# First attention of a transformer block: couples of maxima moved behind the values, the row of maxima by 32-row matmuls, reciprocals in quarters

## The reference

```
x = x + attn(layernorm(x), W_qkv, b_qkv, W_out, b_out)    # H=16 heads of D=64
x = x + ffn(layernorm(x), ...)                            # 16 heads of 8, then 4 experts

def attn(x, ...):
    q, k, v = split(x @ W_qkv + b_qkv)                    # (b, s, 3, H, D)
    k = k + pos_enc
    scores = einsum('bqhd,bkhd->bhqk', q, k) / 8
    out = einsum('bhqk,bkhd->bqhd', softmax(scores), v)
    return out.reshape(b, s, H * D) @ W_out + b_out
```

## Time and profile before

| | |
|---|---|
| median of 3 runs | 2605.41 us |
| the profiled execution | 2604.06 us |
| its span, first to last instruction | 2602.3 us, mean granted TensorE clock 0.969 |
| TensorE matmuls busy | 2437.0 us (94%) |
| VectorE busy | 1970.0 us (76%) |
| ScalarE busy | 1119.5 us (43%) |
| GpSimd busy | 1007.9 us (39%), all of it in the first 1500 us |

### The profile page before, as it was taken

One profiled execution on the slowest core, in us unless ns is written; L12 is line 12 of the kernel. 1 busy time (PEld: TensorE's weight loads), 2 busy tenths in 40 slices (PEclk: granted clock), 3 DMA queues, 4 the chain that ended last, 5 costly groups with the idle time before them and its releaser, 6 DMA issues. The chain is left out here.

```text
span 2602.3 us, 37556 instructions
## 1 busy us (share of the span) xinstructions
PE 2437.0 (94%) x13217; PEld 1300.1 (50%) x13217; DVE 1970.0 (76%) x3109; ACT 1119.5 (43%) x1178; POOL 1007.9 (39%) x459
## 2 busy tenths in 40 slices
PE   5999999999999999999999789999998999999696
PEld 3555454555454555555555344454454455445465
DVE  6767777777767676777777498888987988888834
ACT  0333343333343343443344305556565556655332
POOL 1676767675867767676757600000000000000000
PEclk8999999999999999999999859999999999999898
DMA  2000000000000000000000000000000000000000
GB/s 83 1 1 1 1 1 1 1 1 1 1 1 1 1 1 1 1 1 1 1 1 1 17 8 5 5 12 5 5 8 7 9 8 5 5 5 12 17 0 16
DMA packets 17395, 16.59 MB, mean 6 GB/s; under 512 B 4656, under 2 KB 13760, under 8 KB 17088
## 3 DMA queue, kind: packets, MB, share of 16 engines
q1 hardware_dynamic: 17216, 14.20, 2.0%
HBM read 8.16 MB, written 1.05 MB: 4 GB/s over the span
## 5 line engine op out<-in xcount | busy, mean ns | idle before, releaser
L715 ACT ACTIVATE prob<-scores 128x1024 f32<-128x1024 f32 x512 | 523.9, 1025 | 765.4 <-PE scores L408 717.4
L798 POOL TENSOR_TENSOR accp<-accp,prob 128x1024 f32<-128x1024 f32 x320 | 773.5, 2417 | 71.7 <-ACT prob L715 35.2
L982 DVE TENSOR_REDUCE mxp<-ring 128x1 f32<-128x512 f32 x1024 | 634.9, 680 | 151.5 <-PE ring L383 151.5
L743 ACT ACTIVATE prob<-scores 128x1024 f32<-128x1024 f32 x512 | 496.7, 1022 | 417.5 <-PE scores L567 417.3
L420 PE MATMUL acc_o<-prob,v 128*64 128x512 f32 x2048 | 496.7, 606 | 0.0
L531 PE MATMUL ring<-khi,klo_q 128*128 128x512 f32 x1104 | 450.2, 452 | 8.7 <-DVE accs L1130 3.8
L1107 DVE TENSOR_REDUCE mxp<-ring 128x1 f32<-128x512 f32 x576 | 372.1, 686 | 37.5 <-PE ring L531 37.3
L1107 DVE TENSOR_REDUCE accs<-ring 128x1 f32<-128x512 f32 x528 | 343.6, 687 | 52.9 <-PE ring L531 52.2
L531 PEld LDWEIGHTS ring<-khi,klo_q 128*128 128x128 f32 x1104 | 214.4, 195 | 312.1 <-DVE mxp L1107 132.4
L403 PE MATMUL scores<-klo_q,khi 64*128 64x512 f32 x2048 | 354.5, 418 | 0.0
L567 PE MATMUL scores<-klo_q,khi 128*128 128x512 f32 x1028 | 338.2, 410 | 7.0 <-issue 6.4
(11 more groups left out here) (119 smaller groups left out, 1520.9 us busy)
## 6 DMA issues: line engine op xcount, KB each, us to landing
klo_q<-stage_q SPq DMA_DIRECT2D x72, 64.0 KB, 2.0
w_all<-w_pairs SPq DMA_DIRECT2D x1, 1344.0 KB, 10.6
klo_q<-m_rows SPq DMA_DIRECT2D x68, 2.0 KB
pos_sb<-pos SPq DMA_DIRECT2D x1, 1024.0 KB, 5.9
mrow<-m_rows SPq DMA_DIRECT2D x64, 2.0 KB
v<-w SPq DMA_DIRECT2D x1, 1024.0 KB, 5.2
prob<-w SPq DMA_DIRECT2D x4, 256.0 KB, 3.6
out<-prob SPq DMA_DIRECT2D x4, 256.0 KB, 2.4
```

The costliest lines, as they stand in the source:

```text
L715: nc.scalar.activation(prob[:, T % SLOTS1, :, :], sc[T % 2][:, :, :], ACT.Exp, scale=SCALE1).then_inc(exp_done, 1)
L743: nc.scalar.activation(prob2[:, u, t % 4, :, :], sc[u][:, :, :], ACT.Exp, scale=SCALE2).then_inc(exp2_done[u], 1)
L798: nc.gpsimd.tensor_tensor(accp[:, k % 2], accp[:, k % 2], prob[:, T % SLOTS1], ALU.add).then_inc(pool_acc, 1)
L982: done(nc.vector.reduce_max(mxp1[k % 2][:, h * QT + q, kc:kc + 1], bank[:], AX.X), ("max", k, q, kc, h))
```

## The change

1. `scores(T)` no longer adds the maxima. A new `maxima_off(T)`, called once for two tiles and ahead of them, starts the accumulation of all four banks by four matmuls of 32 rows: `onesw` has ones in rows 0, 32, 64 and 96, and `mrow` holds the row of maxima in those four rows. It waits for the exp of tile T - 1, and at a chunk's first tile for the DMAs of `mrow`, of which there are four now.
2. The second couple of a step is issued behind the values and the item, on both TensorE and VectorE; the order of the ring changes with it.
3. ScalarE copies `sums` to SBUF (`ssum`). VectorE takes the reciprocals from there, 128 columns in each of steps 2 to 5. `normalise` waits for all four and stands behind GpSimd's ninth add.
4. `y` moves from step 6 to step 7, and the K or V item of step 7 to step 6; `split_keys` of step 3 stands behind the eighth add.

```diff
@@ last_item1
-    if j in (3, 7) and k // NC + 1 < PAIRS:
+    if j in (3, 6) and k // NC + 1 < PAIRS:
...
-    if j == 6 and k > 0:
+    if j == 7 and k > 0:
         return ("y", k - 1)
@@ TensorE, scores(T)
-                if T >= 2:
-                    pe.wait_ge(exp_done, T - 1)
...
-                                         start=(n == 0), stop=False)
-                if t == 0:
-                    pe.wait_ge(m_dma, 32 * (k + 1))
-                for h in range(2):
-                    nc.tensor.matmul(sc[u][:, h, :], onesw[half(h), :], mrow[half(h), k % 2, :],
-                                     start=False, stop=True).then_inc(sc_ready[u], 1)
+                                                start=False, stop=(n == 2))
+                        if n == 2:
+                            last.then_inc(sc_ready[u], 1)
+
+            def maxima_off(T):
+                k = T // NT
+                if T >= 2:
+                    pe.wait_ge(exp_done, T)
+                if T % NT == 0:
+                    pe.wait_ge(m_dma, 64 * (k + 1))
+                for u in range(2):
+                    for h in range(2):
+                        rows = slice(64 * h + 32 * u, 64 * h + 32 * u + 32)
+                        nc.tensor.matmul(sc[u][:, h, :], onesw[rows, :], mrow[rows, k % 2, :], start=True, stop=False)
@@ TensorE, the step
+                            if n == 0:
+                                maxima_off(T)
                             scores(T)
-                        cp = couple1(k, j, n)
-                        if cp:
+                        cp = couple1(k, j, 0)
+                        if n == 0 and cp:
                             couple(*cp)
                     values(NT * k + 2 * j)
                     values(NT * k + 2 * j + 1).then_inc(pv_done, 1)
                     it = last_item1(k, j)
                     if it:
                         item1(it)
+                    cp = couple1(k, j, 1)
+                    if cp:
+                        couple(*cp)
@@ ScalarE, behind the exps of a step (j = 1)
+            def sums_copy(k):
+                wait_full(act, ("sums", k))
+                if k > 0:
+                    act.wait_ge(rec_ready, QT * k)
+                nc.scalar.activation(ssum[:], ring[bank_of(("sums", k))][:], ACT.Copy).then_inc(free[...], 1)
@@ GpSimd
             def normalise(k):
                 pool.wait_ge(o_copied, k + 1)
-                wait_free(pool, ("sums", k))
+                pool.wait_ge(rec_ready, QT * (k + 1))
...
-                    if t == 5 and k > 0:
+                    if t == 9 and k > 0:
                         normalise(k - 1)
-                    if t == 9 and last_item1(k, 3) and last_item1(k, 3)[0] == "K":
+                    if t == 8 and last_item1(k, 3) and last_item1(k, 3)[0] == "K":
@@ SyncE
-                for h in range(2):
-                    sp.dma_start(mrow[64 * h:64 * h + 1, k % 2, :].bitcast(F32),
+                for r in range(4):
+                    h = r // 2
+                    sp.dma_start(mrow[32 * r:32 * r + 1, k % 2, :].bitcast(F32),
@@ VectorE
-                nc.vector.reciprocal(rec[:, 0:256], bank[:, 0:256])
-                done(nc.vector.reciprocal(rec[:, 256:512], bank[:, 256:512]), ("sums", k))
+                cols = slice(q * 128, (q + 1) * 128)
+                nc.vector.reciprocal(rec[:, cols], ssum[:, cols]).then_inc(rec_ready, 1)
@@ VectorE, the step
-                        if cp:
+                        cp = couple1(k, j, 0)
+                        if n == 0 and cp:
                             couple(*cp)
+                    if 2 <= j < 2 + QT and k > 0:
+                        reciprocals(k - 1, j - 2)
                     it = last_item1(k, j)
                     if it:
                         item1(it)
+                    cp = couple1(k, j, 1)
+                    if cp:
+                        couple(*cp)
```

More of the change, by code:

```diff
@@ L101, in uses1 @@
         for j in range(STEPS1):
-            for half in range(2):
-                cp = couple1(k, j, half)
-                if cp:
-                    use(("couple", *cp))
+            before, after = couple1(k, j, 0), couple1(k, j, 1)
             it = last_item1(k, j)
-            if it:
-                use(it)
+            for x in (("couple", *before) if before else None, it, ("couple", *after) if after else None):
+                if x:
+                    use(x)
     use(("sums", CHUNKS1 - 1))
@@ L196, in build @@
         oraw = sb("oraw", [128, 2, CW])
+        ssum = sb("ssum", [128, CW])
         rec = sb("rec", [128, CW])
@@ L269, in build @@
         pool_acc, dve_acc = sem("pool_acc"), sem("dve_acc")
-        onorm_ready, row_ready = sem("onorm_ready"), sem("row_ready")
+        rec_ready, onorm_ready, row_ready = sem("rec_ready"), sem("onorm_ready"), sem("row_ready")
         mx_ready, m_dma = sem("mx_ready"), sem("m_dma")
@@ L402, in scores @@
                     for h in range(2):
-                        nc.tensor.matmul(sc[u][:, h, :], of_k[half(h), p % 2, of_keys], of_q[half(h), c, :],
-                                         start=(n == 0), stop=False)
-                if t == 0:
-                    pe.wait_ge(m_dma, 32 * (k + 1))
-                for h in range(2):
-                    nc.tensor.matmul(sc[u][:, h, :], onesw[half(h), :], mrow[half(h), k % 2, :],
-                                     start=False, stop=True).then_inc(sc_ready[u], 1)
+                        last = nc.tensor.matmul(sc[u][:, h, :], of_k[half(h), p % 2, of_keys], of_q[half(h), c, :],
+                                                start=False, stop=(n == 2))
[11 more added lines that the diff above has]
+                        nc.tensor.matmul(sc[u][:, h, :], onesw[rows, :], mrow[rows, k % 2, :], start=True, stop=False)
             def values(T):
@@ L469, in _ @@
                 item1(it)
-            pe.wait_ge(blank, 4)
+            pe.wait_ge(blank, 6)
+            maxima_off(0)
             scores(0)
@@ L704, in v_copy @@
                                      .rearrange("p (t n) -> p t n", t=QT), ACT.Copy).then_inc(free[bank_of(("V", p, b))], 1)
+            def sums_copy(k):
+                wait_full(act, ("sums", k))
+                if k > 0:
+                    act.wait_ge(rec_ready, QT * k)
+                nc.scalar.activation(ssum[:], ring[bank_of(("sums", k))][:], ACT.Copy).then_inc(free[bank_of(("sums", k))], 1)
             def exps(T):
@@ L737, in _ @@
                         v_copy(*it[1:])
+                    elif it and it[0] == "sums":
+                        sums_copy(it[1])
                 copy_o1(k)
+            sums_copy(CHUNKS1 - 1)
             def exps2(G, u, t):
@@ L809, in _ @@
             pool.wait_ge(blank, 2)
-            for h in range(2):
-                nc.gpsimd.memset(onesw[64 * h:64 * h + 1, :].bitcast(F32), 1.0).then_inc(blank, 1)
-                pool.wait_ge(blank, 3 + h)
+            for r in range(4):
+                nc.gpsimd.memset(onesw[32 * r:32 * r + 1, :].bitcast(F32), 1.0).then_inc(blank, 1)
+                pool.wait_ge(blank, 3 + r)
             for b in range(NC):
@@ L817, in _ @@
                     add(NT * k + t)
-                    if t == 5 and k > 0:
+                    if t == 9 and k > 0:
                         normalise(k - 1)
-                    if t == 9 and last_item1(k, 3) and last_item1(k, 3)[0] == "K":
+                    if t == 8 and last_item1(k, 3) and last_item1(k, 3)[0] == "K":
                         split_keys(*last_item1(k, 3)[1:])
-                if last_item1(k, 7) and last_item1(k, 7)[0] == "K":
-                    split_keys(*last_item1(k, 7)[1:])
+                if last_item1(k, 6) and last_item1(k, 6)[0] == "K":
+                    split_keys(*last_item1(k, 6)[1:])
             normalise(CHUNKS1 - 1)
@@ L993, in fin @@
                 if k > 0:
-                    dve.wait_ge(m_dma, 32 * k)
+                    dve.wait_ge(m_dma, 64 * k)
                 bank = open_(("fin", k))
@@ L1012, in add, with reciprocals @@
                 nc.vector.tensor_tensor(accp[:, k % 2], accp[:, k % 2], prob[:, T % SLOTS1], ALU.add).then_inc(dve_acc, 1)
-            def sums(k):
-                bank = open_(("sums", k))
+            def reciprocals(k, q):
+                wait_free(dve, ("sums", k))
                 if k > 0:
                     dve.wait_ge(onorm_ready, k)
-                nc.vector.reciprocal(rec[:, 0:256], bank[:, 0:256])
-                done(nc.vector.reciprocal(rec[:, 256:512], bank[:, 256:512]), ("sums", k))
+                cols = slice(q * 128, (q + 1) * 128)
+                nc.vector.reciprocal(rec[:, cols], ssum[:, cols]).then_inc(rec_ready, 1)
             def y(k):
@@ L1045, in item1 @@
                     fin(it[1])
-                elif kind == "sums":
-                    sums(it[1])
                 elif kind == "y":
@@ L1078, in _ @@
                         item1(it)
+                    cp = couple1(k, j, 1)
+                    if cp:
```

(4 more changed lines are left out.)

## The result

The changed kernel takes 2691.4 us, median of 4 runs (2686.8 to 2700.9), against 2605.0 (2604.1 to 2610.2) before: ratio 1.034, 95% interval 1.032 to 1.035. The profiled execution took 2686.75 us, its span 2684.8. The forecast was 2598, its range 2560 to 2653; even the rival that named what happened (C, 2649) is some 40 us short.

A forecast was written before the change was run, and what follows sets the result against it. TensorE, busy 193 of 200 us, was taken to set the pace. Terms summed to -0.4 us a chunk, times 30 -12; with last chunk, start and tail -7.6: 2596.5 profiled, 2598 us median, range 2560 to 2653.

The forecast's parts named there:

- C: Slower rival: GpSimd wins the 0.07 us at the boundary, VectorE's add 13 waits, in V chunks; 2649 us, chance 0.20.
- the walk through step 7: V chunk's boundary, instruction by instruction: VectorE's add 13 starts at 3.53, GpSimd's first add at 3.60.
- The forecast lead: At a V chunk's boundary: VectorE's add 13 starts 0.07 us ahead of GpSimd's first add.
- Row of maxima: Maxima matmuls, per chunk: -3.68 for slots removed, +1.84 for 32-row groups, +3.2 for row changes; sum +1.36 us.
- The 0.12 of a regular step: Each step: the second couple's 0.12 us wait for its bank goes, -0.96 us a chunk.
- Reciprocals: TensorE's wait behind the reciprocals goes, -1.8 us a chunk; each quarter takes VectorE 0.83 us.
- Q: After a Q item: the next step's first couple waits for its bank, +0.78 us a chunk.
- Boundary: Chunk's boundary, VectorE's and GpSimd's adds: new waits of mean +1.5 us replace today's 1.3.
- B: Faster rival: 64-to-32-row changes cost nothing and the boundary is no worse than walked; 2562 us, chance 0.20.
- D: Slower rival: the four 32-row maxima matmuls go two by two; 2653 us, chance 0.08.
- E: No-change rival: row changes free, but GpSimd leads by 0.3 us at the boundary; 2602 us, chance 0.10.
- F: Slower rival: reciprocals reading and writing SBUF keep GpSimd out, as adds do; 2613 us, chance 0.04.

The follow-up runs named there:

- e8: Kernel of e2 with a step's first couple issued ahead of scores(T), in all steps: 2577.9 us, ratio 0.989 to the kernel before.
- e5: Changed kernel with e1's wait, and maxima by four 64-row matmuls in place of 32-row ones: 2567.9 us, ratio 0.985 to the kernel before.
- e2: Kernel before with only the sums copied to SBUF, reciprocals in quarters in steps 2 to 5 and normalise moved: 2550.8 us, ratio 0.978.
- e1: Changed kernel, but GpSimd's first add of a chunk waits for VectorE's add 13 of the chunk before: 2586.3 us, ratio 0.991 to the kernel before.
- e3: Kernel before with only the maxima by 32-row matmuls, couples where they were: 2656.9 us, ratio 1.019.
- e4: Kernel before with only the second couple moved behind values and item: 2771.2 us, ratio 1.062.
- e11: Changed kernel with couples, y, K and V in their old places, leaving quarters and 32-row maxima: 2586.4 us, ratio 0.993 to the kernel before.
- e12: Changed kernel with y back in step 6 and K or V, with its split_keys, back in step 7: 2629.0 us, ratio 1.009 to the kernel before.

## Why the prediction was wrong

The step that failed is in the walk through step 7: "the exps take 2.17, now end at 3.53 and GpSimd starts at 3.60. VectorE is first by 0.07 us." VectorE's side came as walked: from the second couple of step 6 (628.76) to add 13 (632.30) it is 3.54, forecast 3.53. The exps start 1.36 behind that couple, as the walk has it (3.53 less 2.17), but the two take 1.94:

```profile
630.12 1.94 ACT L733 ACTIVATE prob<-scores 128x1024 f32<-128x1024 f32 x2 [1.19 <-PE scores L400]
```

GpSimd so starts 3.38 behind the couple and not 3.60, and VectorE is later by 0.16. The 2.17 was read where five slots of TensorE lie between the scores of the two tiles (5 x 0.23 = 1.15, more than the 1.02 of one exp, so that ScalarE waits in between); the change itself leaves four (0.92), and the exps run back to back. Behind K chunks, where the key split holds GpSimd, VectorE is later by 0.02 to 0.03.

The forecast lead would have been enough, had it been there. In e8 VectorE is ahead by 0.06 to 0.08 in every V chunk, and no add 13 is lost; VectorE and GpSimd in one of them:

```profile
418.07 1.22 DVE L1024 TENSOR_TENSOR accp<-accp,prob 128x1024 f32<-128x1024 f32 x1
```
```profile
418.15 3.35 POOL L807 TENSOR_TENSOR accp<-prob 128x1024 f32<-128x1024 f32 x1 [2.52 <-ACT prob L724]
```

The walk was off by 0.23 us, which is no use where the answer hangs on 0.07. I should have seen that the change takes VectorE's lead from 0.46 us to about nothing, and given the lost race at least an even chance.

Point by point:
- Row of maxima, +1.36 us a chunk from two changes of 0.20: right (0.43 and 0.44 in the trace, steps 4.55), and e5 confirms the price. It was the wrong bargain already on paper.
- The 0.12 of a regular step gone: right. Reciprocals, -1.8: right; e2 gave 54 us of the 54 expected, though a quarter takes 0.94 and not 0.83.
- Q, +0.78: right; its step is 6.34, where 4.55 and the item's 1.05 make 5.60.
- Boundary, +1.5: in e1, where VectorE is first as assumed, the whole kernel takes 2587.2 profiled against the 2596.5 of the forecast, so that sum was 9 us too high. In the changed kernel the three steps from the values of step 7 to those of step 2 take 20.2 us a chunk together against 16.9 in e1, 3.3 more with the clock's share in it; the term was mis-sized by about that, since a chunk lasts 46.95 where 44.1 was forecast.
- C was priced for V chunks only, 15 x 3.4 = 51 us; by its own price the 25 that were lost make 85, and 2683. In the K chunks I took for granted that VectorE's add goes first at the end of the key split; with add 1 of GpSimd due at the same moment it did not in 9 of 14.
- What no part of the prediction had: TensorE's clock. It falls behind some of the waits of 1 us and more, and that is some 28 of the 90 us between the forecast for the profiled execution (2596.5) and 2686.75. The earlier trace rows showed 1.00, and I took it as a constant.

B, D, E and F are out: changes of rows are not free, the four matmuls run side by side, and GpSimd's adds are not held up by the reciprocals.

## What to carry to other kernels

Where the adds of two engines keep each other out and the first to come goes first, write down each one's lead at every meeting, work it out anew for the changed order (a time read under the old order can hold a wait that the new order lacks), and take a lead smaller than the error of that sum as open; or decide it with a wait, as e1 did: GpSimd idle for 1.3 us more, the kernel 105 us faster. A slot of TensorE saved by smaller row tiles must beat the changes of tiling around it (0.20 us each here), and a slot between two uses of a short ring of banks may be what hides the wait for the bank (e3). Try the parts of a change alone: one of them was worth 54 us and the others hid it.

## What the runs showed of the hardware

- Two changes between 64 and 32 rows, there and back, together with one group of four 32-row matmuls by 512 columns to four banks, cost 0.64 us (4.55 - 4.37 + 0.46). The four start within 0.01 us of each other; if they take one slot of 0.23, a change costs 0.20, as much as one from 128 rows by 64 columns to 64 rows.
- The granted clock fell to 1.2 GHz for short stretches in a kernel that keeps TensorE over 90% busy: 0.98 on average in the changed kernel and e3, 0.96 in e4, 1.00 in e1 and e11, nearly always in or behind a wait of 1.2 to 2.2 us. Not every such wait brings it: 10 of 25 in the changed kernel, 17 of 30 in e3, 1 of 30 before the change. A stall followed by a fall costs more than its own length.
- Adds of VectorE and GpSimd that meet run one after the other. With VectorE 0.01 to 0.03 us behind by the trace it went both ways in one execution: VectorE 3.42 and GpSimd 2.36, or VectorE 1.22 and GpSimd 3.49. VectorE 0.06 to 0.08 ahead always went first (e8), 0.13 and more behind never (changed kernel, e12).
- Reciprocals of 128 columns from SBUF to SBUF do not meet GpSimd's adds in this way: 0.94 to 0.95 us beside an add and without one (e2).
